# CIN recurrence on one core: the broadcast rows x_bc loaded through ScalarE's DMA queue instead of SyncE's

## The reference

```python
for i, f in enumerate([128, 128, 128]):
    Wr = Ws[i].reshape(h, 39, f)                    # h = 39, then 64, then 64
    z = relu(einsum('bhk,bmk,hmf->bfk', prev, x0, Wr) + bs[i][None, :, None])
    results.append(z[:, :64])                       # first half is kept
    prev = z[:, 64:]                                # second half feeds the next layer
y = sum(concatenate(results, axis=1), axis=-1) @ W_lin
```

## Time and profile before

| | |
|---|---|
| median of 3 runs | 2056.39 us (2055.49 to 2056.47) |
| the profiled execution | 2055.68 us |
| its span, first to last instruction | 2053.9 us |
| PE / DVE / ACT busy, share of the span | 99% / 88% / 26% |
| mean granted TensorE clock | 0.997 of full speed |
| moved from memory | 308.74 MB, 150 GB/s over the span |
| one block, from one start of layer 1 to the next | 63.05 us |

### The profile page before, as it was taken

The page is one execution under the profiler, slowest core; times in us unless marked ns, Lnnn a source line. Parts: engine busy times, 40 slices in busy tenths (PEclk is TensorE's granted clock), DMA queues, the critical chain, the costliest instruction groups (busy, mean ns, idle before and its releaser), DMA issues.

```text
span 2053.9 us, 20773 instructions
## 1 busy us (share of the span) xinstructions
PE 2030.3 (99%) x6050; PEld 804.6 (39%) x6050; DVE 1809.6 (88%) x1630; ACT 539.0 (26%) x547; POOL 1.2 (0%) x5
## 2 busy tenths in 40 slices
PE   7999999999999999999999999999999999999998
PEld 2344333443333443334433344333344333443342
DVE  6988988889988889888899888898888988889987
ACT  1331133311333212333113332123321233311322
POOL 0000000000000000000000000000000000000000
PEclk9999999999999999999999999999999999999999
DMA  8967866668766688666786666876668866668710
GB/s 199 199 146 163 179 145 140 148 146 190 158 130 150 144 176 169 150 139 144 157 190 142 140 147 143 187 166 133 147 145 168 183 141 141 145 148 190 152 38 0
DMA packets 98550, 308.99 MB, mean 150 GB/s; under 512 B 19252, under 2 KB 19252, under 8 KB 98408
## 3 DMA queue, kind: packets, MB, share of 16 engines
q1 hardware_dynamic: 97400, 307.71, 68.7%
q10 hardware_dynamic: 1136, 1.12, 0.2%
HBM read 308.74 MB, written 0.01 MB: 150 GB/s over the span
## 4 chain that ended last, share of the span: by engine, by line
PE 89%; DVE 6%; issue 3%; ACT 0%; DVEq 0%
PE acc L323 66%; PE acc L362 20%; DVE prod L210 4%; PE acc L317 3%; DVE prod L212 2%; ACT prev L404 0%; DVE sum L258 0%; DVE x_bc L189 0%; DVEq L241 0%; PE acc_y L393 0%; DVE x_rot L201 0%; ACT res L434 0%; DVE x_seed L305 0%; ACT pool L439 0%; DVEq L240 0%
## 5 line engine op out<-in xcount | busy, mean ns | idle before, releaser
L210 DVE TENSOR_TENSOR prod<-prev,x_bc 128x1024 f32<-128x1024 f32 x1216 | 1390.1, 1223 | 221.6 <-ACT prev L404 215.0
L323 PE MATMUL acc<-prod,w_sb 128*128 128x512 f32 x2432 | 1052.3, 593 | 0.3 <-DVE prod L210 0.3
L323 PEld LDWEIGHTS acc<-prod,w_sb 128*128 128x128 f32 x2432 | 459.4, 190 | 592.6 <-issue 546.8
L362 PE MATMUL acc<-prod,w_sb 128*64 128x512 f32 (+1 forms) x2560 | 569.3, 596 | 6.1 <-DVE prod L212 1.2
L323 PE MATMUL acc<-x_rot,w_sb 117*128 117x512 f32 (+1 forms) x768 | 341.0, 599 | 2.7 <-DVE x_rot L201 2.7
L362 PEld LDWEIGHTS acc<-prod,w_sb 128*64 128x64 f32 (+1 forms) x2560 | 175.3, 136 | 396.2 <-issue 320.1
L409 ACT ACTIVATE prev<-acc,bias 32x1024 f32<-32x1024 f32 x256 | 283.4, 1107 | 4.0
L404 ACT ACTIVATE prev<-acc,bias 64x1024 f32<-64x1024 f32 x128 | 142.0, 1109 | 498.6 <-PE acc L317 355.2
L201 DVE TENSOR_TENSOR x_rot<-x_rot,x_rep 117x1024 f32<-117x1024 f32 (+1 forms) x192 | 221.1, 1220 | 3.0 <-DMA x_rot<-x 2.9
L323 PEld LDWEIGHTS acc<-x_rot,w_sb 117*128 117x128 f32 (+1 forms) x768 | 143.4, 190 | 198.8 <-issue 189.7
L439 ACT ACTIVATE pool<-sum,wl_col 128x64 f32 (+1 forms) x65 | 22.1, 342 | 679.6 <-DVE sum L258 679.6
(11 more groups left out here) (17 smaller groups left out, 21.8 us busy)
## 6 DMA issues: line engine op xcount, KB each, us to landing
x_bc<-x SPq DMA_DIRECT2D x310, 256.0 KB, 13.1
x_bc<-x SPq DMA_DIRECT2D x155, 512.0 KB, 21.2
x_rot<-x SPq DMA_DIRECT2D x192, 312.0 KB
x_rot<-x SPq DMA_DIRECT2D x192, 156.0 KB
x_bc<-x SPq DMA_DIRECT2D x124, 128.0 KB, 8.9
x_rep<-x SPq DMA_DIRECT2D x64, 192.0 KB
x_rep_s<-x SPq DMA_DIRECT2D x64, 128.0 KB, 2.6
x_rot_s<-x SPq DMA_DIRECT2D x64, 128.0 KB, 2.8
```

Source lines behind the costliest of these rows:

```text
L210: mul = nc.vector.tensor_tensor(prod[:, slot, :], old[:], new, ALU.mult)
L323: mm = nc.tensor.matmul(acc[:, h, :], w, rhs[:, BANK * h:BANK * h + BANK], start=start, stop=stop)
L362: mm = nc.tensor.matmul(acc2[HALF * h:HALF * h + HALF, :], w2_sb[0:k, c, :], prod[0:k, c % RING, BANK * h:BANK * h + BANK], start=(c == 0) ...
```

## The change

`load_bc` and the helper that it needs leave SyncE's program and are written into ScalarE's. In the loop ACT waits for the last product of block i and issues the 19 DMAs for block i + 2 between `weigh01(i)` and `evacuate2(i)`. The first `load_bc(1, 1)` comes behind `evacuate0(0)`. SyncE keeps `load_pairs` and its waits for layer 0, and counts up a semaphore that nobody waits for.

```diff
@@ block.sync
-            def load_bc(i, u):
-                ...
             load_pairs(1)
-            load_bc(1, 1)
             for i in range(U):
                 sp.wait_ge(acc0_full, i + 2)
                 load_pairs(i + 2)
-                sp.wait_ge(prod_ready, i * (2 * CH) + 2 * CH)
-                load_bc(i + 2, i)
             with sp.Fori(1, STEPS - 1) as j:
                 for u in range(U):
                     i = j * U + u
                     sp.wait_ge(acc0_full, i + 2)
+                    sp.sem_inc(pairs_asked, 1)
                     load_pairs(i + 2)
-                    sp.wait_ge(prod_ready, i * (2 * CH) + 2 * CH)
-                    load_bc(i + 2, u)
@@ block.scalar
+            def load_bc(i, u):
+
+                for g, (t0, t1) in enumerate(XB_GROUPS):
+                    for q in range(QPT):
+                        src = rows_of(i, QPT * t0 + q, [[0, QUAD], [QPT * NB, t1 - t0], [1, NB]])
+                        act.dma_start(x_bc[QUAD * q:QUAD * q + QUAD, u, t0:t1, :], src).then_inc(bc_loaded[u][g], 16)
+                for q in range(2):
+                    src = rows_of(i, QPT * T + q, [[0, HALF], [1, NB]])
+                    act.dma_start(x_bc[HALF * q:HALF * q + HALF, u, T2, :], src).then_inc(bc_loaded[u][-1], 16)
+                src = rows_of(i, M - 1, [[0, P], [1, NB]])
+                act.dma_start(x_bc[:, u, T1, :], src).then_inc(bc_loaded[u][-1], 16)
             evacuate0(0)
+            load_bc(1, 1)
             with act.Fori(0, STEPS - 1) as j:
                     weigh01(i)
+                    act.wait_ge(prod_ready, i * (2 * CH) + 2 * CH)
+                    load_bc(i + 2, u)
                     evacuate2(i, i * (2 * CH) + 2 * CH)
```

More of the change, by code:

```diff
@@ L103, in cin_kernel @@
                      for u in range(U)]
+        pairs_asked = sem("pairs_asked")
         prod0_ready = sem("prod0_ready")
@@ L448, in weigh2, with rows_of @@
                 weigh(pool2, i * BB, sum2, 1)
+            def rows_of(i, first, ap):
+                base = x[i, first:first + 1, :]
+                return bass.AP(tensor=base.tensor, offset=base.offset, ap=ap)
+            def load_bc(i, u):
[8 more added lines that the diff above has]
+                act.dma_start(x_bc[:, u, T1, :], src).then_inc(bc_loaded[u][-1], 16)
             act.dma_start(w0_sb[:], w0).then_inc(w0_loaded, 16)
```

## The result

The changed kernel takes 2064.9 us (median of 6 runs, 2062.49 to 2065.32) against 2056.43 us (6 runs, 2054.95 to 2056.91): ratio 1.004, 95% interval 1.0028 to 1.0052. It is 8.5 us slower, where the prediction had 2056.5 us and at most 2060.

A forecast was written before the change was run, and what follows sets the result against it. The prediction took a 63.04 us path per block through PE, ACT and DVE as the bound. Its terms summed to 0 per block and 0 to 1 us once, added to the 2056.39 median: 2056.5 us, range 2054 to 2060.

The forecast's parts named there:

- What bounds the kernel, and the slack in the loop: Every block: 63.04 us path through PE, ACT and DVE; DVE's 7.06 us wait for ACT is the slack.
- the cover over `evacuate2`: ACT in each block: evacuate2 ends 7.3 us later, 12.7 us before the channel sum, with DVE's 7.06 us idle behind.
- Nineteen issues on ACT at no cost: Loop, in front of evacuate2: 19 issues at 0.50 us each, 9.51 us on ACT; cost 0.
- ACT becomes the wait: Every block, evacuate2 behind 19 issues: slower from 1.54 us an issue, 2450 us in all at 2.23; chance 0.02.
- a gain from SyncE's freed time: SP idles 38 us between jobs, so gain 0; the rival that SP or the transfers gain had chance 0.04.
- The step that failed: Block 0: ACT issues the broadcast rows when evacuate0(0) ends at 42.56, with 1.47 of 3.96 MB of pair rows moved.
- the share: Block 0: two queues share evenly, so the remaining 2.5 MB of pair rows land by 67.6 to 70.3, before 71.2.
- such a lag: Block 0: 1 to 2 us possible once if a pair-row landing lags its bytes; value taken 0.
- turns by the packet: DMA engines alternate between queues a packet at a time, taken to mean an even split in block 0; 0 to 1 us.
- two queues, and the pairs of block 1 come late: Block 0, once: broadcast rows served wholly first, pairs end at 83.9, time grows 11.7 us to 2068; chance 0.04.
- the 76.3 from which the rival decides: Block 0: a last pair group landing after 76.3 makes the time grow by more than the measurement can't tell from none.
- The range: Whole run: 2054 to 2060 us, 2.5 us below and 3.5 us above the forecast for block 0.

The follow-up runs named there:

- e6: From e1: evacuate2 of each block also waits until PE has used 15 chunks of the next layer 1; 2056.75 us against 2056.78 for the kernel before.
- e7: From e1: evacuate2 of each block also waits until PE has used 18 chunks of the next layer 1; 2170.05 us, ratio 1.055 to the kernel before.
- e1: Changed kernel with load_bc(1, 1) back on SyncE behind load_pairs(1), the loop's issues still on ScalarE; 2054.81 us against 2055.33 for the kernel before.
- e3: Changed kernel where ScalarE waits, before load_bc(1, 1), until the last activation of evacuate0(0) has ended; 2054.71 us against 2055.33 for the kernel before.
- e4: Changed kernel where ScalarE waits, before load_bc(1, 1), until block 1's last pair-row group has landed; 2055.17 us against 2055.33 for the kernel before.
- e9: Changed kernel where SyncE issues 8 of load_bc(1, 1)'s 19 DMAs ahead of load_pairs(1), ScalarE the other 11; 2065.68 us against 2056.31 for the kernel before.
- e5: Kernel before, with SyncE issuing load_bc(1, 1) ahead of load_pairs(1) in one queue; 2067.37 us against 2056.78.
- e2: Kernel before, with only load_bc(1, 1) moved to ScalarE behind evacuate0(0), later broadcast rows staying on SyncE; 2064.55 us against 2055.33.
- e8: Changed kernel with SyncE loading 1.97 MB of w1 ahead of load_pairs(1), beside ScalarE's load_bc(1, 1); 2071.36 us against 2056.94 for the kernel before.

## Why the prediction was wrong

**What bounds the kernel, and the slack in the loop: right.** The path of 63.04 us a block, DVE's idle 7.06 us and the cover over `evacuate2` held, and e6 and e7 measure that cover from both sides. One reading was too wide: the idle of 7.06 us is not that of every block, since in block 0 it is 1.04 us. The working for block 0 used the right one.

**Nineteen issues on ACT at no cost: right.** 10.2 us in place of the 9.5 taken; e1 is level with the kernel before. The rival "ACT becomes the wait" is out, and so is a gain from SyncE's freed time: e1, e3 and e4 all have it, and none is measurably faster.

**The step that failed** is the first of block 0: "Now ACT issues the broadcast rows when its `evacuate0(0)` ends at 41.45 + 1.11 = 42.56". I read the order of the program as an order in time. ScalarE issued the first at 34.97, behind only the second of the seven activations, though in its program all seven stand ahead. Block 0 ran 2.0 us earlier in that profile, so on the scale of the kernel before this is 37.0 in place of 42.56. SyncE had issued pair rows for only 2.3 us by then, and 0.18 MB of them had moved, where the prediction counted on 1.47 MB. e3 restores the assumed moment and nothing else, and the time goes back to that of before: this is shown.

**A term that was mis-sized** is the share. "If the two queues now share evenly" made 0.09 to 0.10 MB/us for the pair rows; they got 2.02 MB in 24 us, 0.084. In the changed kernel 1.02 MB of them had moved by 41 (SyncE's queue, 32.6 to 41), and 2.94 MB were left. At 0.10 these would have landed at 70.4, at 0.09 at 73.7, and at 0.084 at 76.0. DVE could have taken the last group at 69.2 + 1.0 = 70.3 without loss. It took it at 79.04: the last 0.93 MB, from 65 to 77, came at 0.078, and the wait ended 2 us after all but 0.01 MB had moved. The prediction had allowed 1 to 2 us for such a lag. So by this working the real start with the prediction's own share costs 0 to 3 us, and the smaller share and the lag make the rest of the 8.7; no run separates them.

The prediction took turns by the packet and an even split to be one case. e9's 181 and 182 packets bear out the turns, but even turns are not an even share: the half-width rows were shorter, and the pieces of 39 partitions had fewer packets in the same time.

**Luck at the assumed start.** With 2.5 MB left at 42.56 and the real 0.084 MB/us, the pair rows would have landed at 72.3, right at the 72.2 that DVE can stand. In e3 they had time to spare because ScalarE's queue came up slowly: from 41 to 47 they still moved 1.06 MB. So that block 0 is free in e3 owes something to a behaviour that the prediction did not have.

**The rival** "two queues, and the pairs of block 1 come late" named the right place, the right work that waits, and a bound of 11.7 us that e5 measures at 10.6 us (2067.37 - 2056.78). It was priced for broadcast rows served wholly first, and that did not happen: the queues shared, and the early start made the pair rows late. It was given 4 in 100, because at an even split from the assumed start the sum had it out of reach. The landing in the changed kernel at 79.0 on its own scale would be 81.0 on the scale of the kernel before, beyond the 76.3 from which the rival decides.

**The range** ended at 2060 because I took the bound of block 0 only from the assumed start. A bound from both sides for the moment of issue, the early one at the wait for `acc0_full`, would have put the loss into view.

**Open:** why ScalarE's queue comes up slowly when it joins a queue that is already full. In e3 it had only 10.4% of the engines' time from 41 to 47 and 37.4% from 47 to 53, though its issues began at 42.60; in the changed kernel it had 36.5% already from 35 to 41. No run here shows the reason. Open too is how far ahead of its activations ScalarE can issue at most: in e2, e8 and e9, as in the changed kernel, the first issue came 0.01 us after the start of the third activation, and no run varies what stands in front.

## What to carry to other kernels

A DMA in ScalarE's program was not held by the activations in front of it here; if one must not start before they have run, or must not run beside another transfer, give it a semaphore to wait for. When a load is moved to a second queue, what is lost is the order between it and what stood ahead of it in the old queue: look for the place where the later of the two was needed late and the earlier one soon. Here that was the start of the program and not its loop. A place that is executed once still costs what it costs: one call made 8.5 us here, and thirty like it nothing.

## What the runs showed of the hardware

DMA issues on ScalarE's queue ran 5.6 us ahead of the activations that precede them: first issue at 34.97, last of these activations from 39.45 to 40.56. A wait for the last of them moved the first issue to 42.60 (e3). Two queues with like transfers shared the DMA engines at 50.2% and 52.3% (e9, one run, one window of 6 us); pair rows in pieces of 39 partitions against broadcast rows shared at 41.1% and 61.9%. Rows of 2 KiB against rows of 4 KiB went at 181 and 182 packets in 4 us, 33.4% and 69.9% of the time (e9, 46 to 50). A plain load of 128 partitions moved at 336 GB/s (e8, 36 to 40, its start included), while the copies of one row to 32 partitions moved at 216 GB/s with all engines busy.
